# Layer-0 attentions in units of two key chunks, with one ring of six PSUM banks and the softmax division inside a PSUM bank

## The reference

```
x = attn(ln(x), ln(x)) @ Wo1 + bo1 + x        # self, 512 keys
x = attn(ln(x), context) @ Wo2 + bo2 + x      # cross, 1601 keys
x = geglu(ln(x)) + x
attn: softmax(q k^T * scale) v, per head
```

## Time and profile before

| | us |
|---|---|
| median of 3 runs (lowest, highest) | 3945.47 (3943.59, 3948.19) |
| the profiled execution: its own time | 3965.1 |
| its span, first to last instruction | 3963.3 |
| mean granted TensorE clock | 0.926 of full |
| a0 and a1 within the span, about | 196 to 611, 1022 to 2192 |
| TensorE busy | 3460.7 |

### The profile page before, as it was taken

The page is one execution under the profiler, slowest core; times in us unless marked ns, Lnnn a source line. Parts: engine busy times, 40 slices in busy tenths (PEclk is TensorE's granted clock), DMA queues, the critical chain, the costliest instruction groups (busy, mean ns, idle before and its releaser), DMA issues. The chain is left out here.

```text
span 3963.3 us, 57945 instructions
## 1 busy us (share of the span) xinstructions
PE 3460.7 (87%) x17596; PEld 1999.5 (50%) x17596; DVE 2427.7 (61%) x4148; ACT 1998.9 (50%) x3541; POOL 1124.3 (28%) x539
## 2 busy tenths in 40 slices
PE   7899995999799999999999588588488599999676
PEld 5644443888455555555554466433366444444254
DVE  4368884443477776777766444386254399999233
ACT  4356662444255555555555223167344168888633
POOL 0056660000366667666677000012000000000000
PEclk8999997999799999999999799789799789999888
DMA  6787867999855555555552423234454512222111
GB/s 212 266 194 194 194 160 253 337 316 309 215 135 130 124 124 138 134 130 124 124 137 52 157 95 111 80 112 133 149 186 147 148 65 96 100 101 101 68 69 43
DMA packets 361056, 590.63 MB, mean 149 GB/s; under 512 B 41242, under 2 KB 194426, under 8 KB 359782
## 3 DMA queue, kind: packets, MB, share of 16 engines
q1 hardware_dynamic: 359944, 586.05, 51.2%
q10 hardware_dynamic: 958, 2.62, 0.3%
HBM read 345.71 MB, written 239.97 MB: 148 GB/s over the span
## 5 line engine op out<-in xcount | busy, mean ns | idle before, releaser
L1198 DVE TENSOR_REDUCE a_blk_max<-a_mx 128x1 f32<-128x402 f32 (+1 forms) x1280 | 733.4, 586 | 431.2 <-PE a_mx L1001 412.3
L1148 ACT ACTIVATE a_prob<-a_sc 128x512 f32<-128x512 f32 (+1 forms) x1088 | 639.7, 596 | 505.6 <-PE a_sc L1030 469.6
L1596 ACT ACTIVATE a_prob<-a_ring 128x512 f32<-128x512 f32 (+1 forms) x1088 | 583.0, 604 | 125.9 <-PE a_ring L1519 120.9
L977 POOL TENSOR_TENSOR a_prob_sum<-a_prob,a_prob_sum 128x1024 f32<-128x1024 f32 x256 | 617.0, 2411 | 63.6 <-ACT a_prob L1148 54.4
L1041 PE MATMUL a_pv<-a_prob,a_v 128*64 128x512 f32 (+1 forms) x2176 | 586.0, 617 | 0.0
L1623 DVE TENSOR_REDUCE a_blk_max<-a_ring 128x1 f32<-128x402 f32 x1024 | 507.2, 566 | 65.9 <-PE a_ring L1506 58.7
L1001 PE MATMUL a_mx<-a_k_stack,a_q_stack 128*128 128x402 f32 (+1 forms) x1280 | 484.9, 389 | 36.8 <-DMA a_q_stack<-q_hi_cross 22.2
L1029 PE MATMUL a_sc<-a_q_stack,a_k_stack 128*128 128x512 f32 (+1 forms) x1088 | 461.0, 424 | 2.1 <-ACT a_q_second L1131 2.1
L1030 PE MATMUL a_sc<-a_q_second,a_k_second 65*128 65x512 f32 (+1 forms) x1088 | 432.2, 397 | 0.0
L977 POOL TENSOR_TENSOR a_prob_sum<-a_prob 128x1024 f32<-128x1024 f32 x128 | 312.0, 2448 | 417.3 <-ACT a_prob L1148 417.3
L1001 PEld LDWEIGHTS a_mx<-a_k_stack,a_q_stack 128*128 128x128 f32 x1280 | 247.8, 194 | 290.2 <-DVE a_blk_max L1198 109.6
(11 more groups left out here) (248 smaller groups left out, 4919.5 us busy)
## 6 DMA issues: line engine op xcount, KB each, us to landing
a_v<-v_cross SPq DMA_DIRECT2D x48, 768.0 KB
a_k_stack<-k_hi_cross SPq DMA_DIRECT2D x32, 801.0 KB, 6.7
a_k_stack<-k_lo_cross SPq DMA_DIRECT2D x32, 801.0 KB, 9.8
a_k_second<-k_hi_cross SPq DMA_DIRECT2D x32, 801.0 KB
v_cross<-p_v_sb SPq DMA_DIRECT2D x48, 512.0 KB, 4.1
k_hi_cross<-p_split_hi SPq DMA_DIRECT2D x120, 200.0 KB, 3.3
k_lo_cross<-p_split_lo SPq DMA_DIRECT2D x120, 200.0 KB, 3.2
a_q_stack<-q_hi_self SPq DMA_DIRECT2D x64, 256.0 KB, 4.8
```

Of the source, the lines that this page charges most:

```text
L977: nc.gpsimd.tensor_tensor(prob_sum[:, h], prob_of(c, cp, h), other, ALU.add)\
L1148: nc.scalar.activation(prob_of(c, cp, h)[0:rows, k, :], sc[0:rows, (c * E + e) % SCB, :], ACT.Exp, scale=a.scale).then_inc(exp_done, 1)
L1198: nc.vector.reduce_max(blk_max[:, r, h, t, nb:nb + 1], mx[:, (c * NI + n) % MXB, 0:a.blk], AX.X)\
L1596: nc.scalar.activation(prob[0:keys, tau % RC, m, :], ring[0:keys, score_place(e) % BANKS, :], ACT.Exp, scale=a.scale).then_inc(exp_done, 1)
```

## The change

`attend_phase` goes, and a0 and a1 are built by a new `attend_wide`. The layer-1 phases, the projections and the arithmetic are as before. What is different in a0 and a1:

* A unit is now a pair of chunks with both heads: four scores, some pairs of maxima, the values of the pair of chunks of the unit before (in one block of up to four fp32 matmuls), in some units the denominators, and in cross the last two pairs of maxima behind the values.
* Scores and maxima share one ring of six banks in the order in which TensorE writes them; the maxima run up to LEAD = 3 units further ahead than before.
* The maxima's columns are turned by VectorE (32 x 32 blocks), stored in DRAM and loaded into the row of q_second; the row of k_second holds -1. TensorE and ScalarE take no part.
* The denominators have a PSUM bank of their own, `sums`. VectorE turns it into SBUF, inverts 16 columns, turns them back, spread over 32 rows, into `sums`, and divides in place there; ScalarE and VectorE take high and low part from it.
* Self attention has 5 slots instead of 4. The k stack is loaded in four pieces of 64 rows instead of two, in the second head with low and high parts exchanged. In cross the last sum and the joining are one instruction each for both heads.

```diff
-def attend_phase(pr, name, a):
...
+def attend_wide(pr, name, a):
+    pr.start_phase()
+    NC, NCP, KP, S, NB, NG = a.NC, a.NCP, a.kp, a.keys, a.NB, a.NG
+    SLOTS = 3 if a.cross else 5
+    RC = 3 if a.cross else 4
+    OS = 3 if a.cross else 4
+    PAIRS = 4 * NB
+    NI = 2 * PAIRS
+    E = 2 * NC
+    BANKS = 6
+    LEAD = 3
+    T = NG * NCP
...
+    DEN_AT = NCP + 2
+    HIGH_AT = DEN_AT + (3 if a.cross else 1)
+    SUM_AT, MERGE_AT = 2 * NCP + 1, 2 * NCP + 3
+    TURN_AT, INVERT_AT, DIVIDE_AT, LOW_AT = (2 * DEN_AT + n for n in ((1, 3, 5, 7) if a.cross else (0, 1, 1, 3)))
+    pool_sums = [(cp, h) for cp in range(1, min(NCP, 6)) for h in range(2)]
+    dve_sums = [(cp, h) for cp in range(6, NCP) for h in range(2)]
+    def pairs_by(w):
+        return min(NG * PAIRS, -(-PAIRS * (NCP + min(LEAD, w + 1) + w + 1) // NCP))
+    def cut(w):
+        return max(pairs_by(w - 1), pairs_by(w) - 2) if a.cross else pairs_by(w)
+    def bank_order():
+        blocks = [(True, g) for g in range(2 * pairs_by(-1))]
+        for w in range(T):
+            i, cp = divmod(w, NCP)
+            blocks += [(False, step_of(i, cp, ch % 2, h)) for ch in a.pair(cp) for h in range(2)]
+            blocks += [(True, g) for g in range(2 * pairs_by(w - 1), 2 * pairs_by(w))]
+        return blocks
+    def step_of(i, cp, k, h):
+        return i * E + 4 * cp + 2 * k + h
...
+            def load_kq(n):
+                s = n % SLOTS
+                if n >= SLOTS:
+                    sp.wait_ge(st_done, (n - SLOTS + 1) * E)
+                (k_hi, k_lo), q_hi = (t[n] for t in pr.k[a.name]), pr.q[a.name][0][n]
+                for h in range(2):
+                    for half, part in enumerate((k_hi, k_lo) if h == 0 else (k_lo, k_hi)):
+                        sp.dma_start(words(kst[s][64 * half:64 * half + 64, h]), part[64 * h:64 * h + 64])\
+                            .then_inc(loaded[s], 16)
+                for half in range(2):
+                    sp.dma_start(words(qst[s][64 * half:64 * half + 64]), q_hi.rearrange("(h r) s -> r h s", h=2))\
+                        .then_inc(loaded[s], 16)
+            def load_second(n):
+                s, k_hi, q_lo = n % SLOTS, pr.k[a.name][0][n], pr.q[a.name][1][n]
+                for dst, src in ((k2[s], k_hi), (q2[s], q_lo)):
+                    sp.dma_start(words(dst[0:64]), src.rearrange("(h r) s -> r h s", h=2)).then_inc(loaded2[s], 16)
...
+            def load_v(n):
+                s, vs, full = n % SLOTS, pr.v[a.name][n], NC - (LAST < P)
+                if n >= SLOTS:
+                    sp.wait_ge(pv_done, (n - SLOTS + 1) * NC)
+                sp.dma_start(v[s][:, 0:full, :], vs[:, 0:full, :]).then_inc(v_loaded[s], 16)
+                if full < NC:
+                    sp.dma_start(v[s][0:LAST, full:NC, :], vs[0:LAST, full:NC, :]).then_inc(v_loaded[s], 16)
+            def store_maxima(n):
+                sp.wait_ge(turned, n + 1)
+                if n >= 2:
+                    sp.wait_ge(row_loaded[n % 2], 16 * (n // 2))
+                sp.dma_start(pr.maxima[n % 2].rearrange("c (b i) -> b c i", b=4), row_turned[:, n % 2, :])\
+                    .then_inc(max_stored[n % 2], 16)
+            def load_maxima(n):
+                sp.wait_ge(max_stored[n % 2], 16 * (n // 2 + 1))
+                sp.dma_start(words(q2[n % SLOTS][64:65]), pr.maxima[n % 2][0:8].rearrange("(o h t) i -> o h (t i)", o=1, h=2))\
+                    .then_inc(row_loaded[n % 2], 16)
...
+            load_kq(0)
+            load_second(0)
+            load_kq(1)
+            load_v(0)
+            store_maxima(0)
+            load_maxima(0)
+            load_second(1)
+            load_v(1)
+            for n in range(2, SLOTS - 1):
+                load_kq(n)
+                load_second(n)
+                load_v(n)
+            for i in range(NG + 3):
+                if a.cross:
+                    at(load_kq, i + SLOTS - 1)
+                    at(load_second, i + SLOTS - 1)
+                    at(load_v, i + SLOTS - 1)
+                    at(store_maxima, i + 1)
+                    at(load_maxima, i + 1)
+                    at(store, i - 1)
+                else:
+                    at(store_maxima, i + 1)
+                    at(load_maxima, i + 1)
+                    at(load_kq, i + SLOTS - 1)
+                    at(load_second, i + SLOTS - 1)
+                    at(load_v, i + SLOTS - 1)
+                    at(store, i - 3)
...
+            def add(i, m):
+                cp, h = pool_sums[m]
+                pool.wait_ge(exp_done, step_of(i, cp, 1, h) + 1)
+                if cp == 1:
+                    if i:
+                        pool.wait_ge(merged, 2 * i if dve_sums else (i - 1) * 2 + h + 1)
+                    other = prob_of(i * NCP, h)
+                else:
+                    pool.wait_ge(pool_sum, i * len(pool_sums) + m - 1)
+                    other = prob_sum[:, h]
+                nc.gpsimd.tensor_tensor(prob_sum[:, h], prob_of(i * NCP + cp, h), other, ALU.add)\
+                    .then_inc(pool_sum, 1)
+            def merge(i, h):
+                pool.wait_ge(pool_sum, i * 2 + h + 1)
+                if i >= CS:
+                    pool.wait_ge(den_done, i - CS + 1)
+                nc.gpsimd.tensor_tensor(chunk_sum[:, i % CS, h, :], prob_sum[:, h, 0, :], prob_sum[:, h, 1, :], ALU.add)\
+                    .then_inc(merged, 1)
+            for i in range(NG):
+                for m in range(len(pool_sums)):
+                    add(i, m)
+                    if not dve_sums:
+                        merge(i, m)
...
+            def bank_free(block):
+                n = place[block]
+                if n >= BANKS:
+                    of_maxima, m = users[n - BANKS]
+                    pe.wait_ge(item_read if of_maxima else exp_done, m + 1)
...
+            def denominators(i):
+                pe.wait_ge(merged, 2 * (i + 1))
+                if i:
+                    pe.wait_ge(o_lo_done, i)
+                for h in range(2):
+                    last = nc.tensor.matmul(sums[64 * h:64 * h + 64, :], pr.ones[:, 0:64],
+                                            chunk_sum[:, i % CS, h, :], start=True, stop=True)
+                last.then_inc(den_done, 1)
+            def values(w):
+                i, cp = divmod(w, NCP)
+                for ch in a.pair(cp):
+                    if ch == 0:
+                        pe.wait_ge(v_loaded[i % SLOTS], 16 * NV * (i // SLOTS + 1))
+                        if i:
+                            pe.wait_ge(pv_copied, i)
+                    pe.wait_ge(exp_done, step_of(i, cp, ch % 2, 1) + 1)
+                    keys = a.chunk_rows(ch)
+                    for h in range(2):
+                        last = nc.tensor.matmul(pv[64 * h:64 * h + 64, :], v[i % SLOTS][0:keys, ch, 64 * h:64 * h + 64],
+                                                prob_of(w, h)[0:keys, ch % 2, :], start=(ch == 0), stop=(ch == NC - 1))
+                    last.then_inc(pv_done, 1)
+            def sums_at(w):
+                if w >= DEN_AT and (w - DEN_AT) % NCP == 0 and (w - DEN_AT) // NCP < NG:
+                    denominators((w - DEN_AT) // NCP)
+            maxima(0, pairs_by(-1))
+            for w in range(T):
+                for ch in a.pair(w % NCP):
+                    for h in range(2):
+                        scores(w, ch % 2, h)
+                maxima(pairs_by(w - 1), cut(w))
+                if w:
+                    values(w - 1)
+                sums_at(w)
+                maxima(cut(w), pairs_by(w))
+            values(T - 1)
+            for w in range(T, T + DEN_AT):
...
+            def prob_free(w, h):
+                i, cp = divmod(w, NCP)
+                act.wait_ge(pv_done, i * NC + min(NC, 2 * cp + 2))
+                one = (max(cp, 1), h)
+                if one in pool_sums:
+                    act.wait_ge(pool_sum, i * len(pool_sums) + pool_sums.index(one) + 1)
+                else:
+                    act.wait_ge(dve_sum, i + 1)
...
+            def turn_sums(i):
+                dve.wait_ge(den_done, i + 1)
+                nc.vector.transpose(den[:], sums[:]).then_inc(sums_turned, 1)
+            def invert(i):
+                dve.wait_ge(sums_turned, i + 1)
+                nc.vector.reciprocal(inv_cols[:], den[:].rearrange("p (k i) -> p k i", i=32)[:, :, 0])\
+                    .then_inc(inverted, 1)
+                dve.wait_ge(inverted, i + 1)
+                nc.vector.transpose(sums[:], inv_cols[:].rearrange("p (k o) -> p k o", o=1).to_broadcast([P, 16, 32]))\
+                    .then_inc(inv_turned, 1)
+            def last_sum(i):
+                cp = NCP - 1
+                rows = a.chunk_rows(2 * cp)
+                dve.wait_ge(exp_done, step_of(i, cp, 0, 1) + 1)
+                dve.wait_ge(pool_sum, (i + 1) * len(pool_sums))
+                nc.vector.tensor_tensor(prob_sum[0:rows, :, 0, :], prob_sum[0:rows, :, 0, :],
```

(39 more changed lines are left out.)

580 lines of the change are left out of this document (146 added, 434 removed).

## The result

The changed kernel takes 3881.51 us (median of 4 runs, 3878.91 to 3885.37) where the kernel before takes 3946.83 (4 runs, 3943.59 to 3953.13): 65.3 us less, ratio 0.9833, 95% interval 0.9816 to 0.985. The prediction said 3861, range 3800 to 3910. The profiled execution took 3885.4 us (span 3883.6), against 3965.1 before. Both are themselves off their medians, by 4 and by 18 us, so the profiled pair differs by 79.7; the stages, not the totals, are to be compared.

The account below looks back on a forecast made before the run. TensorE was taken to bound both attentions before, with self becoming bound by SyncE and DMA; self +4 and cross -89 made -85 us, which from the median 3945.5 gave 3861, range 3800 to 3910.

Parts of the forecast that it names:

- The likeliest case: Self bound by SyncE and DMA, cross at TensorE's new pace: total -85 us, range 3840 to 3891; chance 53%.
- TensorE needs 10.6 and 32.4 us: TensorE's time per group falls from 12.18 to 10.6 us in self and from 35.36 to 32.4 in cross.
- The mergers: Values of two chunks run as one TensorE block: 0.35 us saved each, 2 a group in self, 6 in cross.
- the rows: Transposes for the rows of maxima leave TensorE: 0.44 us saved twice a group, 0.88 us.
- Cross -89: Cross attention: 32 x 2.98 = -95 us, first trip +4, end +2, together -89.
- The loop of GpSimd: In cross, GpSimd's additions, last sum, merge and semaphores take 31.3 us, under TensorE's 32.4; not binding, by 1.1 us.
- Self +4: Self attention: start +11 us, 24 groups +3, last three groups -7.5, end -2.5, together +4.
- The chain: In self, batch 10.9 us, landing of maxima 0.7, issue of load 0.55: taken as 12.3 us a group.
- rival 2: In cross, GpSimd's additions wait for exponentials and its loop binds at 33.8 us: total -39, 3906; chance 16%.
- Divide and low part 0.7 each: VectorE's divide and low part, with one operand in PSUM, take 0.7 us each; the old divide's median was 0.97.
- Rival 1: The maxima's DMA trip is hidden in self too, 10.6 us a group: total -140, 3805; chance 16%.
- Rival 3: VectorE's 512-column transposes cost 3.4 us each: self +58, cross +154, total +127, 4073; chance 8%.

Follow-up runs that it names:

- sp_order: Changed kernel, but in self attention SyncE stores the maxima one group earlier, ahead of the next batch of loads: 3826.8 us, ratio 0.9688 to the kernel before.
- cross alone: Cross attention built the new way, self attention by the old function: 3869.4 us, ratio 0.9793 to the kernel before.
- pool_extra: Changed kernel, but in cross attention GpSimd makes one more sum of 128 x 512 a group inside its loop: 3887.4 us, ratio 0.9834 to the kernel before.
- turns_x5: Changed kernel, but each of the two 512-column transposes of a group is done five times, in self and cross: 4158.4 us.
- values_split: Changed kernel, but in cross values of a unit's two chunks were to stand apart; only one block a group was cut: 3897.9 us.
- merge_late: Changed kernel, but in cross attention VectorE's joining of the sums and all behind it comes one unit (4.65 us) later: 4033.6 us.
- values_apart: Changed kernel, but in cross every unit's values stand apart, one block before all its maxima and one behind: 3950.0 us, ratio 0.9992 to the kernel before.

## Why the prediction was right

The likeliest case came true: self bound by SyncE and DMA, cross at TensorE's new pace. 3881.5 lies 20 us above the 3861, inside the range of the likeliest case (3840 to 3891). Most of the 20 is one term, self attention, which was put at +4 and measured +16; cross is 3 to 7 us short of its -89.

* *TensorE needs 10.6 and 32.4 us.* Right: 10.58 in sp_order and 32.52. The mergers gave 0.347 each (0.35), the rows 0.77 a group (0.88, by subtraction).
* *Cross -89.* Traces -86, median of cross alone -82. The loop of GpSimd stays outside, by at least 1.04 us, and its 36.0 us with one unit more were met in the groups at full clock (35.84 and 35.99). That is the sum of the loop's terms, not each term: 0 was put for the wait ahead of the last sum, which is 3.1 us.
* *Self +4.* This is the term that was mis-sized, with the right mechanism: +16 in the trace, +17 by the median. The prediction had +11 at the fifth group, +3 over the stretch and -10 at the end; the trace has +17.5, +12.5 and -13.9. First, the period was taken as 12.3; it is 12.6 (denominators from 298.0 to 574.7, 22 groups). The chain was batch 10.9 to 11.25, landing 0.7, issue 0.55. The landing was right (316.4 to 317.1), and the last issue only 0.3, but the batch takes 11.5 us (304.88 to 316.4). Second, over the stretch up to the last groups it made 12 us instead of 3, as the gap before the last five groups was 15.9 us long. Third, the fifth group came some 17 us later than before, not 11; some 3 of these only say that the denominators stand a quarter of a group later in the new order. The end won back 14 us, not 10.
* *The batch is longer.* By 0.6 us, where I had allowed 0 to 0.35 for the k stacks in four pieces. The strip above averages 162 GB/s over the nine slices from 306.0 us, with a DMA share of 0.63; the first nine of the kernel before average 230, with a share of 0.96. So the DMA engines lack work at the start of the batch. That the pace of issuing explains it isn't shown: pieces of 128 KB, each 0.6 us of issuing, could bring 218 GB/s. No run had the k stacks in two pieces again, so the cause stays open.
* *What the profile would show.* TensorE under 90% busy, SyncE waiting on the store in every group, transposes of 0.7 us (0.71 and 0.73): right. TensorE's idle time released by the DMA: not as the view has it, which names no releaser ("issue"). ScalarE waiting for a_prob_sum was named as the sign of rival 2: the wait is there (24.6 us in 28 times) without the rival, so the sign was a bad one; TensorE's idle time would have told. DMA share above 0.8: wrong, 0.72. The same bytes over a longer period must give a smaller share; the engines stand idle while SyncE's trip is under way.
* *Divide and low part 0.7 each.* Right, and steady: 684 to 697 ns, and 680 to 693 for the low part, where the old divide ran from 691 to 2712. The Trainium skill, "SBUF — State Buffer", section "Who interferes with whom", says that an instruction of VectorE with at most one input in SBUF does not contend with GpSimd. The steady times agree with that, though no run took the operand's place apart from the rest of the change.
* *Rival 1 (trip hidden)* did not come true by itself, but sp_order made it so with one change of order: 3827 against the 3805 that it was given. The period was right; self gained 39.5 us in the trace (375.1 against 414.6) and not 51, as the start is dearer (TensorE is idle for 5.75, then 3.1 and 2.4 us in the first groups; the first denominators come 15.8 us later than before), and the cross phase gave 82 to 87 instead of 89.
* *Rival 2 (GpSimd)* out, by the period of 32.52 and by pool_extra. *Rival 3* out by the measured 0.71 us, but its price was judged by load alone in self; in turns_x5 it was two and a half times as dear (+148 instead of +58), with the order of ScalarE's instructions and a lower clock behind it.

## What to carry to other kernels

When an engine's queue waits for the completion of its own small transfer before it issues the next batch, the period is the batch's bytes plus the trip, even if each engine has time to spare (12.6 us here, with TensorE busy 88% and a DMA share of 0.72); issue the store, then the next batch, and the dependent load behind it (here 55 us of 3,881). A change over two phases should be read phase by phase: a gain of 82 us hid a loss of 17. Do not take a wait in a trace for a bound before asking whether the bounding engine stands idle for it: ScalarE's 24.6 us cost nothing. And look at a trace of the experiment before believing its time: values_split had changed one unit in seven.

## What was not expected of the hardware

* A store of 16 KB on ScalarE's own queue took 10.4 us to its dependent load while SyncE's queue was full, and 2.0 us on SyncE's queue when the loads ahead of it had ended.
* TensorE stood idle for 29.6 of 250 us in self, 0.2 to 2.2 us ahead of a group's scores, and its mean granted clock over that stretch was 0.95 of full speed; it was 1.00 without the idle time (sp_order). In merge_late the same shows group by group: at 0.91 of full speed a group took 2.4 to 3.3 us longer than at full clock.
* One fp32 value block (four half-width instructions) set apart costs TensorE 0.347 us with not a moment of idle time on the busy count: both orders show 100.00 of 100 us, and 433 against 406 instructions in them. A busy share of 100% says nothing of the work done.

```profile
1300.00:1400.00 100.00, 100.00 (x406) 49.26 (x403) 63.56 (x122) 41.57 (x80) 66.30 (x29) 1.00 0.57 134
```

(values_apart; the changed kernel's row is the second of the windows shown first.)
